# Two layer norms of an attention and expert-mixture block: their application moved from ScalarE to VectorE, the small steps on GpSimd cut to one, and a fold reordered

## The reference

```
pooled = x.reshape(B, 12, 14, 16, 14, 16).sum(axis=(3, 5))       # 224 x 224 pixels, 12 channels
h = concat([einsum('bcij,ce->bije', pooled, channel_weights).reshape(B, 196, 192), txt], axis=1)
h = h + attention(layernorm(h))        # 12 heads of 16, rotary positions, causal, a sink column
h = h + experts(layernorm(h))          # 2 of 8 experts per token, capacity 1.25, SwiGLU of 512
layernorm(v) = (v - mean(v)) / sqrt(var(v) + 1e-5)               # over the 192 columns
```

## Time and profile before

| | us |
|---|---|
| median of three runs | 3116.91 |
| lowest and highest of them | 3115.43, 3157.16 |
| the profiled execution, its own time | 3111.47 |
| its span (first to last instruction) | 3109.3 |

### The profile page before, as it was taken

The page is one execution under the profiler, slowest core; times in us unless marked ns, Lnnn a source line. Parts: engine busy times, 40 slices in busy tenths (PEclk is TensorE's granted clock), DMA queues, the critical chain, the costliest instruction groups (busy, mean ns, idle before and its releaser), DMA issues.

```text
span 3109.3 us, 62400 instructions
## 1 busy us (share of the span) xinstructions
PE 2852.4 (92%) x20432; PEld 2539.9 (82%) x20432; DVE 1827.3 (59%) x5319; ACT 1497.5 (48%) x3736; POOL 2019.5 (65%) x2070
## 2 busy tenths in 40 slices
PE   1899999999999999999999985999999999999997
PEld 0788888888888888888878875989898989888997
DVE  2466766676676766677766753444444545444544
ACT  0455555555555555555555553444443444344433
POOL 2567877777777777777777742555565555555555
PEclk9899999999999999999999997999999999999999
DMA  6354445433444433444433303343333343433343
GB/s 182 131 165 156 152 162 172 146 101 101 114 115 115 108 95 104 115 115 115 110 96 102 84 23 74 54 68 48 68 54 68 47 68 54 67 49 66 54 67 44
DMA packets 205961, 297.49 MB, mean 96 GB/s; under 512 B 88374, under 2 KB 167675, under 8 KB 205874
## 3 DMA queue, kind: packets, MB, share of 16 engines
q1 hardware_dynamic: 82994, 243.82, 27.4%
q0 software_dynamic: 122880, 52.55, 12.0%
HBM read 201.73 MB, written 93.90 MB: 95 GB/s over the span
## 4 chain that ended last, share of the span: by engine, by line
PE 32%; issue 22%; POOL 19%; DMA 14%; DVE 6%; ACT 4%; POOLq 1%; DVEq 1%; SPq 0%; ACTq 0%
DMA out<-arena,who 13%; POOL out L1460 10%; PE bank L861 6%; POOL moe_rows L1281 5%; PE bank L979 3%; PE bank L927 3%; DVE arena L1442 3%; PE bank L952 2%; PE bank L954 2%; PE bank L905 2%; PE bank L1029 2%; POOL rstd L706 2%; PE bank L963 1%; PE bank L852 1%; PE bank L929 1%
## 5 line engine op out<-in xcount | busy, mean ns | idle before, releaser
L1460 POOL DMA_INDIRECT out<-arena,who x320 | 596.1, 1863 | 187.4 <-issue 183.2
L1281 POOL DMA_INDIRECT moe_rows<-row,slot x256 | 293.2, 1145 | 349.0 <-issue 324.8
L570 DVE TENSOR_REDUCE top<-bank 114x2 f32<-114x456 f32 (+1 forms) x576 | 352.9, 622 | 240.9 <-PE bank L921 153.4
L1418 ACT ACTIVATE arena<-bank 128x456 f32<-128x456 f32 x320 | 174.9, 547 | 602.4 <-PE bank L1409 600.8
L685 POOL TENSOR_TENSOR arena<-arena 112x896 f32<-112x896 f32 x192 | 402.2, 2096 | 44.4 <-DMA arena<-in_x 44.4
L1432 PE MATMUL bank<-prob,arena 128*114 128x192 f32 x2560 | 429.3, 326 | 0.0
L1432 PEld LDWEIGHTS bank<-prob,arena 128*114 128x114 f32 x2560 | 412.2, 178 | 0.0
L1424 DVE TENSOR_TENSOR arena<-bank,arena 128x456 f32<-128x456 f32 x320 | 201.5, 630 | 209.3 <-ACT arena L1418 207.3
L1449 POOL TENSOR_TENSOR rms<-rms,minus_half 114x4 f32<-114x4 f32 x82 | 85.3, 1040 | 345.3 <-DVE rms L1347 345.3
L725 POOL TENSOR_TENSOR qk<-rot_c,qk 114x384 fp32r<-114x384 f32 x256 | 253.7, 1014 | 44.4 <-ACT qk L746 44.4
L547 ACT ACTIVATE pieces<-bank 64x456 fp32r<-64x456 f32 x384 | 209.2, 545 | 149.3 <-PE bank L905 147.1
(11 more groups left out here) (167 smaller groups left out, 6971.3 us busy)
## 6 DMA issues: line engine op xcount, KB each, us to landing
arena<-in_x SPq DMA_DIRECT2D x64, 2352.0 KB, 11.6
arena<-moe_rows SPq DMA_DIRECT2D x82, 363.4 KB
moe_rows<-filler SPq DMA_DIRECT2D x20, 1453.5 KB
out<-h SPq DMA_DIRECT2D x64, 171.0 KB
out<-arena,who POOLq DMA_INDIRECT x320, 5.0
arena<-in_w_t SPq DMA_DIRECT2D x9, 512.0 KB, 6.7
arena<-in_w_t SPq DMA_DIRECT2D x18, 256.0 KB, 7.1
moe_rows<-row,slot POOLq DMA_INDIRECT x256, 4.1
```

Source lines behind the costliest of these rows:

```text
L570: nc.vector.tensor_reduce(dst, src, AX.X, ALU.max).then_inc(maxed[k], 1)
L1281: nc.gpsimd.indirect_dma_start(out=moe_rows[0:SLOTS, :], out_offset=bass.IndirectOffsetOnAxis(ap=slot[at.par][:, 2 * t + k:2 * t + k + 1], ...
L1460: nc.gpsimd.indirect_dma_start(out=out[:, :], out_offset=bass.IndirectOffsetOnAxis(ap=who[par][:, s:s + 1], axis=0), in_=ys[par][:, s, :], ...
```

## The change

Both norms are applied by VectorE, as (value - mean) x rstd in one operation per half, with mean and rstd read per row. ScalarE's two applies go. GpSimd keeps only the power; the addition of eps moves to VectorE, behind the aggregation; `scaled` and `shifted` with their constants go. In VectorE's queue `norm1_apply` stands behind the first maximum, ahead of the residual; `norm2_apply` stands behind the third maximum, ahead of `pool_image` 0. In GpSimd's queue fold 0 moves from ahead of norm 2's power to behind it.

```diff
         def row_stats(dve, at, src, norm):
...
             for t in range(2):
                 ins = nc.vector.bn_aggr(mv[:, t, :], stats[:, t, :])
             ins.then_inc(step, 1)
+            dve.wait_ge(step, 4 * at.b + 2)
+            nc.vector.tensor_scalar(var[:, :], mv[:, :, 1:2].rearrange("p a b -> p (a b)"), LN_EPS, None,
+                                    ALU.add).then_inc(step, 1)
...
+        def norm1_apply(dve, at):
+            dve.wait_ge(ln1_step, 4 * (at.b + 1))
+            wait(dve, xn_turned, at.b)
+            for t in range(2):
+                ins = nc.vector.tensor_scalar(xn[:, t, :, 0:C], h[at.par][:, t, :].rearrange("p (c k) -> p c k", c=2),
+                                              mv1[:, t, 0:1], rstd1[:, t:t + 1], ALU.subtract, ALU.mult)
+            ins.then_inc(ln1_done, 1)
+
+        def norm2_apply(dve, at):
+            dve.wait_ge(ln2_step, 4 * (at.b + 1))
+            wait(dve, scattered[at.par], 64 * at.half)
+            for t in range(2):
+                ins = nc.vector.tensor_scalar(row[at.par][:, t, 0:D], h2[at.par][:, t, :],
+                                              mv2[:, t, 0:1], rstd2[:, t:t + 1], ALU.subtract, ALU.mult)
+            ins.then_inc(ln2_done, 1)
...
         def inverse_std(pool, at, norm):
...
-            pool.wait_ge(step, 6 * at.b + 2)
+            pool.wait_ge(step, 4 * at.b + 3)
             wait(pool, done, at.b)
-            nc.gpsimd.tensor_tensor(var[:, :], spread2, ln_eps[:, 0:2], ALU.add).then_inc(step, 1)
-            pool.wait_ge(step, 6 * at.b + 3)
             nc.gpsimd.tensor_tensor(rstd[:, :], var[:, :], minus_half[:, 0:2], ALU.pow).then_inc(step, 1)
-            pool.wait_ge(step, 6 * at.b + 4)
-            nc.gpsimd.tensor_tensor(scaled[:, :], mean, rstd[:, :], ALU.mult).then_inc(step, 1)
-            pool.wait_ge(step, 6 * at.b + 5)
-            nc.gpsimd.tensor_tensor(shifted[:, :], zeros2[:, :], scaled[:, :], ALU.subtract).then_inc(step, 1)
...
             maxima("0")
+            if a:
+                norm1_apply(dve, a)
             if z:
                 residual(dve, z)
                 norm2_stats(dve, z)
             maxima("1 2")
+            if z:
+                norm2_apply(dve, z)
             if p:
                 pool_image(dve, p, 0)
...
                 if a:
                     inverse_std(pool, a, norm1)
-                if p:
-                    fold_image(pool, p, 0)
                 if z:
                     inverse_std(pool, z, norm2)
                 if p:
+                    fold_image(pool, p, 0)
                     fold_image(pool, p, 1)
```

More of the change, by code:

```diff
@@ L162, in build @@
         minus_half = sb("minus_half", [TT, 4])
-        ln_eps = sb("ln_eps", [TT, 2])
-        zeros2 = sb("zeros2", [TT, 2])
         before = sb("before", [TT, TT], bf16)
@@ L193, in build @@
         rstd1 = sb("rstd1", [TT, 2])
-        scaled1 = sb("scaled1", [TT, 2])
-        shifted1 = sb("shifted1", [TT, 2])
         var1 = sb("var1", [TT, 2])
@@ L230, in build @@
         rstd2 = sb("rstd2", [TT, 2])
-        scaled2 = sb("scaled2", [TT, 2])
-        shifted2 = sb("shifted2", [TT, 2])
         var2 = sb("var2", [TT, 2])
@@ L432, in setup_vector @@
             nc.vector.memset(minus_half[:, :], -0.5)
-            nc.vector.memset(ln_eps[:, :], LN_EPS)
-            nc.vector.memset(zeros2[:, :], 0.0)
             nc.vector.memset(w_out[:, :, :], 0.0).then_inc(cleared, 1)
@@ L504, in pool_image @@
             ins.then_inc(x_pooled, 1)
-        norm1 = (st1, mv1, var1, scaled1, rstd1, shifted1, ln1_step, ln1_done)
-        norm2 = (st2, mv2, var2, scaled2, rstd2, shifted2, ln2_step, ln2_done)
+        norm1 = (st1, mv1, var1, rstd1, ln1_step, ln1_done)
+        norm2 = (st2, mv2, var2, rstd2, ln2_step, ln2_done)
         def row_stats(dve, at, src, norm):
-            stats, mv, _, _, _, _, step, _ = norm
-            wait(dve, step, 6 * at.b)
+            stats, mv, var, _, step, _ = norm
+            wait(dve, step, 4 * at.b)
             for t in range(2):
@@ L515, in row_stats @@
             ins.then_inc(step, 1)
-            hold(dve, step, 6 * at.b + 1, held)
+            hold(dve, step, 4 * at.b + 1, held)
             for t in range(2):
@@ L698, in inverse_std @@
         def inverse_std(pool, at, norm):
-            _, mv, var, scaled, rstd, shifted, step, done = norm
-            mean, spread2 = (mv[:, :, i:i + 1].rearrange("p a b -> p (a b)") for i in range(2))
-            pool.wait_ge(step, 6 * at.b + 2)
+            _, _, var, rstd, step, done = norm
+            pool.wait_ge(step, 4 * at.b + 3)
             wait(pool, done, at.b)
-            nc.gpsimd.tensor_tensor(var[:, :], spread2, ln_eps[:, 0:2], ALU.add).then_inc(step, 1)
-            pool.wait_ge(step, 6 * at.b + 3)
             nc.gpsimd.tensor_tensor(rstd[:, :], var[:, :], minus_half[:, 0:2], ALU.pow).then_inc(step, 1)
-            pool.wait_ge(step, 6 * at.b + 4)
-            nc.gpsimd.tensor_tensor(scaled[:, :], mean, rstd[:, :], ALU.mult).then_inc(step, 1)
-            pool.wait_ge(step, 6 * at.b + 5)
-            nc.gpsimd.tensor_tensor(shifted[:, :], zeros2[:, :], scaled[:, :], ALU.subtract).then_inc(step, 1)
         def add_rotation(pool, at, t):
@@ L755, in copy_h @@
             nc.scalar.activation(h[at.par][0:IMG1, 1, :], bank[6][0:IMG1, D:2 * D], ACT.Copy).then_inc(h_copied, 1)
[L757 to L771, removed]
         def keep_h(act, at):
@@ L1105, in step_scalar @@
             exps("0")
-            if a:
-                norm1_apply(act, a)
             exps("1 2")
@@ L1111, in step_scalar @@
             exps("3")
-            if z:
-                norm2_apply(act, z)
             exps("4")
```

## The result

The changed kernel takes 3549.84 us (median) against 3116.68 of the kernel before: 1.1353 times, 95% interval 1.1258 to 1.1447. It is slower, as forecast, but by 433 us instead of 213, and above the range, which ended at 3375. (The kernel before was timed again beside the experiments; its medians lie between 3104 and 3124 us, so ratios to the kernel before of the same session are the safer figures, and differences between sessions are good to some 20 us. The ratios compare means of undisturbed runs, so they differ a little from the quotient of two medians.) The profiled execution took 3555.83 us, its span is 3554.0.

The account below looks back on a forecast made before the run. No engine is simply full; a loop through several engines sets the pace. 162 us (60 steps of 2.7) plus 51 for the clock, +213 on 3111.5, is 3325, and 5 more for the median gives 3330 us; range 3155 to 3375.

Parts of the forecast that it names:

- case B: Apply 2 beside the folds: its halves wait for fold 0 and fold 1, 2.7 us later per step; chance 0.50.
- A: Rival: both halves of apply 2 go together after fold 0, 1.0 us later per step, 3198 us; chance 0.27.
- the order's 0.6 us per step: Fold 0 behind norm 2's power delays `pool_image` 0, `rotate` 0 and `make_qk` 1; `turn_qk` comes 0.6 us later.
- case C: Rival: no contention of apply 2 with the folds, only 0.6 us later per step, 3164 us; chance 0.16.
- 2.7 us per step, 162 us in all: `make_qk` 1 starts later by 2.6 + 0.13 us in each of 60 steps with all five batches in flight.
- the clock term: TensorE's clock falls after its waits in 40 steps, 32 more than before, at 1.6 us each: 51 us.
- B with a slow spell in every step: Both halves of apply 2 wait for folds and TensorE's clock falls in all 60 steps: 3362 us.
- The faster rival, D: GpSimd's order doesn't bind, `turn_xn`'s 1.25 us gain arrives at `turn_qk`: 3029 us; chance 0.04.

Follow-up runs that it names:

- E6: Changed kernel with GpSimd's old order (fold 0 between the two norms' powers), each fold waiting for the norm's halves ahead of it: 3072.39 us, 0.9892 of before.
- E2: Changed kernel with one wait more: GpSimd starts fold 1 only when norm 2 has been applied: 3435.88 us, 1.1004 times before.
- E10: Changed kernel with norm 2 applied by ScalarE again and 8 extra matmuls of 456 columns ahead of `make_qk` 1: 3146.12 us, 1.0132 times before.
- E5: Kernel before with only fold 0 moved behind norm 2's four small GpSimd steps: 3117.28 us, 1.0036 times before.
- E7: Changed kernel with unread matmuls of 456 columns, 10 ahead of `turn_xf` and 7 ahead of `make_qk` 1: 3272.58 us, 1.0532 times before.
- E4: Changed kernel with GpSimd's old order, fold 0 between the two norms' powers, applies still on VectorE: 3266.25 us, 1.0485 times before.
- E1: Changed kernel with unread matmuls of 56 columns, 16 ahead of `turn_xf` and 12 ahead of `make_qk` 1: 3541.95 us, 1.128 times before.

## Why the prediction was right in its mechanism and wrong in its size

**Right: apply 2 waits for a whole fold per half (case B).** The median of the halves of `row` is 1982 ns, against 371 for the shortest. E6 shows that it is the folds: with them held back no half is long; E2 that the second half's wait is for fold 1. The rule that the prediction drew from the Trainium skill, page SBUF — State Buffer, section Who interferes with whom, is that a two-port VectorE operation and a GpSimd operation exclude each other on the shared ports. The trace agrees for the operation itself, which the trace before didn't contain: 1.98 us beside a fold, its end 0.12 behind the fold's. That the ports are the reason, no run shows by itself. Between B and A the prediction chose on rows of scatters: with fold 1 queued behind fold 0, the second half waits for fold 1 too. That held.

**Right: the order's 0.6 us per step (case C's share).** E10 leaves nearly just that: no half of `row` on VectorE, clock full. Its steps of 27.92 us are 0.61 over the mean of 27.31; the kernel is 42 us slower than before, and the prediction had 36. E5 sharpens the reason in one point: without VectorE's wait the swap of fold 0 costs 9 us.

**Right: 2.7 us per step, 162 us in all, at the full clock.** E7 takes the low clock away and leaves the rest, and has 3272.58 us, 164.7 above its own kernel before. Its steps of 29.9 us are 2.6 over 27.31.

**Wrong: the clock term.** The step that failed is "I take 40, so 32 more, 51 us". What remains of 433 us after E7's 165 is 268 us, five times the term. Both its factors were too small. The count: of 37 steps between 506 and 1792 us of the changed kernel, by the starts of norm 1's power, only 4 are as short as 29.8 us, the length at full clock; 33 of 37 would be some 54 of 60, not 40. The price: those 33 steps take 35.4 us on the mean, 5.5 more than E7's, where the prediction had 1.6; the step shown takes 38.5, 8.6 more. E2 shows 6.0 more at 0.80 within one kernel. An estimate from these two, 54 times 5.5, is some 300 us, of the size of the 268. The 1.6 was read from steps of before at 0.94, in which the low clock ended soon; in the step shown it lasts 22.8 us. Taking the price of a short spell for that of any spell, and bounding only the count (8 to 60) but not the price, is why even B with a slow spell in every step, at 3362, stayed below 3375. The rows of before had no long spell, so the price needed an upper bound of its own, and one stood there: PE's 25.3 us of work in a step last that much longer if all of it runs at half the clock. In the step shown most of it did, and the range should have allowed for that.

A reading behind the term doesn't hold either. The prediction has all six slow steps of before behind a wait of 1.8 us at `turn_xn`. Two of them stand behind shorter ones, such as this step (its wait, then the step as a stretch), and ten steps with a wait of 1.8 or more kept the full clock, the one of the earlier trace rows among them:

```profile
1092.40 0.94 PE L852 MATMUL bank<-ident,xn 114*97 114x114 f32 x4 [1.44 <-ACT xn L761]
```
```profile
1089.66:1118.71 29.05, 27.25 (x222) 23.85 (x221) 19.55 (x59) 15.52 (x35) 20.91 (x27) 0.94 0.40 103
```

**The faster rival, D,** had its premise wrong: norm 2's power is done at 3.94, not by 2.7, and fold 0 at 6.01, not by 4.8. But a part of its gain exists: E6 has 35 of the 88 us that D would have brought, once the folds are made to wait.

**Still open:** what decides in a given step whether the clock falls. It isn't the length of the wait ahead of it alone: in E2 `make_qk` 1 waits 1.42 us in a step at 1.00 and in one at 0.80, and in E4 the clock falls behind a wait of 1.92 us at `turn_xn` and stays behind one of 1.96. Open too is why a spell is short in one kernel and long in another. That filling the waits with work keeps the clock up is shown twice (E7, E10).

## What to carry to other kernels

Before work is moved from ScalarE to VectorE, look at what GpSimd runs at that moment: a VectorE operation on SBUF of 0.37 us that becomes ready beside GpSimd operations of 2 us waits for one of them per instruction, and making the GpSimd operation wait 0.8 us for it can be cheaper than not waiting (E6 against E4: 0.989 of before against 1.049). Where a new wait on TensorE arises in a loop like this one, with TensorE over 90% busy, price it twice: once for its own length and once for a stretch at the lower clock behind it, with the whole loop's TensorE work as the bound of the second. To tell the two apart on the chip, fill the wait with matmuls that nobody reads; here those of 456 columns did it and those of 56 did not.

## What the runs showed of the hardware

The low clock can outlast the waits ahead of it by far: in the step shown of the change it is 0.50 for 22.8 us, from inside the second of two waits of 1.90 and 1.42 us, with PE 96% busy in that time. In E4 a fall behind a wait of 1.92 us cost no time at all (29.91 us against 29.84). Matmuls of 56 columns in the change's waits (E1) left time and clock as they were, matmuls of 456 columns (E7) kept the clock at 1.00, and the added work paid back 277 us. And where the fold had started first, the blocking shows on VectorE alone: two folds back to back held one VectorE half each to 0.12 us behind the fold's end, while the folds themselves took 4.15 us for both, against 2.08 and 2.09 before. An operation as small as 114x2 is held too (E6: 0.67 us instead of 0.17).
